# A six-part decoder on one core: three bias additions as TensorE products with a row of ones, the gated experts copied out of PSUM by ScalarE, and softplus compensation without a scale

## The reference, cut to what matters

```python
# L0_ffn: two dense experts, each kept where the gate's top-2 picks it
e0 = silu(x @ w0.T + b0); e1 = silu(x @ w1.T + b1)
out = e0 * fw[:, 0:1] * m0 + e1 * fw[:, 1:2] * m1
# L1_attn: state-space mixer
projected = h @ in_proj_w.T + in_proj_b;  x, z = split(projected, 2)
x = silu(conv(x) + conv_b);  dt, Bc, Cc = split(x @ x_proj_w.T, ...)
dt = softplus(dt @ dt_proj_w.T + dt_proj_b)
decay = floor(exp(dt * A) * 2**15) / 2**15          # 512 channels x 16 states
h = decay * h + (x * Bc) * dt                       # scan over 256 positions
y = (h * Cc).sum(states) + x * D;  y = y * silu(z)
out = y @ out_proj_w.T + out_proj_b
# L1_xattn: 8 heads of 64 against a context of 256 positions
out = softmax(q @ k.T * scale) @ v @ Wo + bo
```

## Time and profile before

| what | value |
|---|---|
| median of 3 runs | 2634.4 us (2625.34 to 2636.75) |
| profiled execution | 2631.68 us, its span 2629.8 us |
| TensorE matmul busy over the span | 2168.8 us (82%), 11024 instructions |
| VectorE busy | 1634.4 us (62%) |
| ScalarE busy | 1030.7 us (39%) |
| GpSimd busy | 289.7 us (11%) |
| mean granted TensorE clock | 0.890 |

### The profile page before, as it was taken

One profiled execution on the slowest core, in us unless ns is written; L12 is line 12 of the kernel. 1 busy time (PEld: TensorE's weight loads), 2 busy tenths in 40 slices (PEclk: granted clock), 3 DMA queues, 4 the chain that ended last, 5 costly groups with the idle time before them and its releaser, 6 DMA issues. The chain is left out here.

```text
span 2629.8 us, 31266 instructions
## 1 busy us (share of the span) xinstructions
PE 2168.8 (82%) x11024; PEld 1327.3 (50%) x11024; DVE 1634.4 (62%) x2717; ACT 1030.7 (39%) x1611; POOL 289.7 (11%) x332
## 2 busy tenths in 40 slices
PE   6999999999999988754668887977888778749994
PEld 4666666666666655431323344434444434536662
DVE  6555555555555566447999999999999952120002
ACT  1222222222222222115765867587668712212220
POOL 1111111111111111100000000010000002110005
PEclk8999999999999999867779987988899876559997
DMA  6000100010001000010110111111001120003333
GB/s 219 1 0 17 46 2 0 17 41 8 0 17 41 7 0 0 1 40 33 54 49 23 47 40 38 34 38 37 27 33 55 48 68 30 15 19 100 100 100 112
DMA packets 57469, 102.55 MB, mean 39 GB/s; under 512 B 7828, under 2 KB 39087, under 8 KB 56832
## 3 DMA queue, kind: packets, MB, share of 16 engines
q1 hardware_dynamic: 54272, 93.67, 10.8%
q0 software_dynamic: 3072, 7.28, 0.9%
HBM read 87.10 MB, written 14.94 MB: 39 GB/s over the span
## 5 line engine op out<-in xcount | busy, mean ns | idle before, releaser
L1788 PE MATMUL pa<-arena 128*128 128x512 f32 x512 | 306.4, 728 | 97.7 <-DVE arena L1363 97.5
L1355 DVE TENSOR_TENSOR_SCAN arena<-arena 128x1024 f32<-128x1024 f32 x128 | 292.3, 2284 | 8.4 <-ACT arena L813 8.0
L1576 PE MATMUL po<-arena 128*128 128x256 f32 x1024 | 230.1, 381 | 0.0
L1566 PE MATMUL pa<-arena 128*128 128x512 f32 x512 | 227.9, 598 | 0.8 <-ACT arena L661 0.8
L1788 PEld LDWEIGHTS pa<-arena 128*128 128x128 f32 x512 | 103.4, 221 | 228.8 <-DVE arena L1363 127.5
L676 ACT COPY arena<-po 128x512 f32<-128x512 f32 x64 | 37.5, 586 | 462.6 <-PE po L1531 462.6
L1576 PEld LDWEIGHTS po<-arena 128*128 128x128 f32 x1024 | 191.2, 189 | 31.9 <-issue 3.5
L528 POOL TENSOR_SCALAR arena<-arena 128x2 f32<-128x2 f32 (+1 forms) x92 | 27.5, 299 | 1602.4 <-DVE arena L1222 932.0
L797 ACT ACTIVATE arena<-arena 128x510 f32<-128x510 f32 x256 | 170.4, 716 | 59.1 <-DVE arena L1355 51.5
L1497 PE MATMUL po<-arena 128*128 128x128 f32 x492 | 94.0, 326 | 117.5 <-ACT arena L824 74.9
L1052 DVE TENSOR_TENSOR arena<-pa,arena 128x512 f32<-128x512 f32 x256 | 158.4, 681 | 25.9 <-PE pa L1511 25.0
(11 more groups left out here) (254 smaller groups left out, 3701.0 us busy)
## 6 DMA issues: line engine op xcount, KB each, us to landing
arena<-bc_rows SPq DMA_DIRECT2D x64, 512.0 KB, 4.4
arena<-in_L_ffn_W SPq DMA_DIRECT2D x16, 1024.0 KB, 7.3
arena<-in_L_attn_W SPq DMA_DIRECT2D x8, 1024.0 KB, 5.2
rows_to_experts<-arena SPq DMA_DIRECT2D x4, 1024.0 KB, 12.6
arena<-rows_to_experts SPq DMA_DIRECT2D x8, 512.0 KB, 8.5
rows_from_experts<-arena SPq DMA_DIRECT2D x8, 512.0 KB, 3.3
arena<-in_x SPq DMA_DIRECT2D x4, 512.0 KB, 6.8
arena<-in_rows SPq DMA_DIRECT2D x8, 256.0 KB, 3.2
```

What stands on the lines that cost most here:

```text
L1355: v.tensor_tensor_scan(h.rearrange(flat), decay.rearrange(flat), h.rearrange(flat), 0.0, ALU.mult, ALU.add).then_inc(scan_done, 1)
L1566: last = mm(pa[(i + 2) % 4][:, :], w1[:, k, ts(i, P)], yT[:, k, :], start=k == 0, stop=k == KC - 1)
L1576: last = mm(po[s][:, ts(i, D)], gT[:, c, ts(2 * s + i, P)], w2[:, c, :], start=c == 0, stop=c == FM - 1)
L1788: last = mm(pa[c][:, :], ident, uh[i % len(uh)][:, n, :], start=g == 0 and n == 0, stop=g == NS // NG - 1 and n == NG - 1)
```

## The change

TensorE gets a helper `biased`, a product of one row of ones with one row of the bias, which opens an accumulation; the products that follow add to it. It is used for the gated experts, the output projection and `w_o`. VectorE's three bias additions go. The experts' PSUM tile is now copied out by ScalarE in slots 15 to 18, so the table `HEAD` has five As where it had Vs, and silu waits for all four copies. Waits on the semaphore `xc_ready` become waits on `proj_added`. In softplus the correction is subtracted as it is; the factor 0.5 e - 1 and the product with it go (two operations over 128 x 2048), and the last operation subtracts instead of adding.

```diff
-HEAD = "AAAAAAVVAAVVVVVAA"
+HEAD = "AAAAAAVVAAVAAAAAA"
@@ SyncE
-        sp.wait_ge(xc_ready, PAIRS)
+        sp.wait_ge(proj_added, 2 * PAIRS)
@@ ScalarE
+            def expert_out(i):
+                nc.scalar.copy(eb[:, i, :], part(11 + i)).then_inc(head_a, 1)
+
             def experts_silu():
+                act.wait_ge(head_a, HEAD_A * n + 12)
                 for i in range(TT):
-                    act.wait_ge(head_v, HEAD_V * n + 4 + i)
                     a_(eb[:, i, :], eb[:, i, :], ACT.Silu).then_inc(sil_ready, 1)
...
+                if 15 <= i < 19:
+                    expert_out(i - 15)
                 if i == 19:
                     experts_silu()
@@ VectorE
-            def pair_biased(i):
-                v.tensor_tensor(eb[:, i, :], part(11 + i), r_pair, ALU.add).then_inc(head_v, 1)
...
-                step.after(v.tensor_scalar(soft_r, soft_e, 0.5, -1.0, ALU.mult, ALU.add))
                 dve.wait_ge(soft_u_ready, 2 * n + 2)
                 step.after(v.scalar_tensor_tensor(soft_e, soft_d, 1.0, soft_e, ALU.subtract, ALU.subtract))
-                step.after(v.tensor_tensor(soft_e, soft_e, soft_r, ALU.mult))
                 dve.wait_ge(relu_ready, IC * n + IC)
-                step.after(v.tensor_tensor(dt, dt, soft_e, ALU.add))
+                step.after(v.tensor_tensor(dt, dt, soft_e, ALU.subtract))
...
-                dve.wait_ge(proj_added, 2 * p + 2)
-                v.tensor_tensor(pair, pair, wide(r_out, TT), ALU.add).then_inc(xc_ready, 1)
-                hold(dve, xc_ready, p + 1)
+                hold(dve, proj_added, 2 * p + 2)
                 statistics(rows)
             if q is not None:
                 cross(UNITS + 3)
-                dve.wait_ge(wo2_out, 4 * q + 4)
-                step.apart(v.tensor_tensor(xst[:, ts(q, TT), :], xst[:, ts(q, TT), :], wide(r_xo, TT), ALU.add))
...
             if q is not None:
+                hold(dve, wo2_out, 4 * q + 4)
                 statistics(rows_of(q))
@@ TensorE
+        def biased(bank, bias):
+
+            mm(bank, ones[0:1, :], bias[0:1, :], start=True, stop=False)
...
             def expert_pair(i):
                 bank = part(11 + i)
+                biased(bank, r_pair)
                 for c in range(KC):
-                    last = mm(bank, xnT[:, c, ts(i, P)], w_pair[:, c, :], start=c == 0, stop=c == KC - 1)
+                    last = mm(bank, xnT[:, c, ts(i, P)], w_pair[:, c, :], start=False, stop=c == KC - 1)
...
                     pe.wait_ge(at2T_out, 4 * q + tile + 1)
                     pe.wait_ge(pexp_ready, 16 * q + min(4 * tile + 6, 16))
+                    biased(bank_score[:, 0:D], r_xo)
                     for c in range(QC):
-                        last = mm(bank_score[:, 0:D], at2T[:, c, :], w_o[:, c, :], start=c == 0, stop=c == QC - 1)
+                        last = mm(bank_score[:, 0:D], at2T[:, c, :], w_o[:, c, :], start=False, stop=c == QC - 1)
...
                     for i in range(2):
+                        biased(proj_banks[s][:, ts(i, D)], r_out)
                         for c in range(IC):
-                            last = mm(proj_banks[s][:, ts(i, D)], dtx[:, c, ts(2 * s + i, P)], w_out[:, c, :], start=c == 0, stop=c == IC - 1)
+                            last = mm(proj_banks[s][:, ts(i, D)], dtx[:, c, ts(2 * s + i, P)], w_out[:, c, :], start=False, stop=c == IC - 1)
```

More of the change, by code:

```diff
@@ L48 @@
 END_STEPS = 5
-HEAD_STEPS, TAIL_STEPS, CROSS_STEPS = 47, 5, 22
+HEAD_STEPS, TAIL_STEPS, CROSS_STEPS = 45, 5, 21
 ACT_STEPS = 2 * UNITS
@@ L292, in decoder @@
     xpad = arena[:, units_at:units_at + IC * 2 * (S + KCONV - 1)].rearrange("p (c s t) -> p c s t", c=IC, s=2)
-    soft_e, soft_l, soft_d, soft_r = chunks_at(units_at), chunks_at(units_at + IC * W), dtx, chunks_at(late + 2 * NG * W)
+    soft_e, soft_l, soft_d = chunks_at(units_at), chunks_at(units_at + IC * W), dtx
     qT, kT, vv = a(QC, W), a(QC, W), a(TT, QI)
@@ L360, in decoder @@
     w_in_2, ctx_in, a_exp, a_ready = sem("w_in_2"), sem("ctx_in"), sem("a_exp"), sem("a_ready")
-    xn_ready, xc_ready, xf_kept = sem("xn_ready"), sem("xc_ready"), sem("xf_kept")
+    xn_ready, xf_kept = sem("xn_ready"), sem("xf_kept")
     ctxn_in, head_done, head_a, head_v = sem("ctxn_in"), sem("head_done"), sem("head_a"), sem("head_v")
@@ L1298, in head @@
                     gate_logits()
-                if i == 14:
-                    pair_biased(0)
                 if i == 15:
                     gate_weights()
-                    pair_biased(1)
-                if i in (16, 17):
-                    pair_biased(i - 14)
                 if i == 19:
@@ L1334, in cross @@
                     if tile == 0:
-                        dve.wait_ge(xc_ready, q + 1)
+                        dve.wait_ge(proj_added, 2 * q + 2)
                     v.tensor_tensor(row_of, bank_score[:, 0:D], row_of, ALU.add).then_inc(wo2_out, 1)
@@ L1423, in mixer @@
             if p is not None:
-                rows, pair = rows_of(p), xst[:, ts(p, TT), :]
+                rows = rows_of(p)
                 for s in range(2):
```

## The result

| | before | changed |
|---|---|---|
| median, 10 runs each | 2636.0 us (nine from 2625.3 to 2640.9, one of 6986.5) | 2652.5 us (2640.0 to 2659.4) |
| ratio, 95% interval | | 1.0058 (1.0034 to 1.0081) |
| profiled span | 2629.8 us | 2638.2 us |
| VectorE busy | 1634.4 us | 1603.4 us |
| TensorE busy, instructions | 2168.8 us, 11024 | 2207.6 us, 11120 |

What follows compares the result with a forecast made beforehand. VectorE bounds within a scan, the TensorE-ScalarE chain between scans. Pass terms 1.9 - 1.7 + 0 + 1.9 + 0.3 + 1.3 = +3.7 us on 2634.4 gave 2638; forecast 2637 us, range 2612 to 2649.

Steps and rivals of the forecast that it cites:

- The price of a bias product: On TensorE, a one-row product costs 0.93 us for 512 columns, 0.45 for 256, twice that at the lower clock.
- the terms that the products make: Parts of the pass sums that fall away if bias products are free: 14.8 us in all, 2.6 of it in pass 6.
- Pass 1, +1.9: Head with nothing beside it: additions start 5.4 us later behind copies and table load, softplus gives back 3.55; sum +1.9 us.
- the TensorE term of 3.5 us: Pass 1: eight more instructions for the experts, 0.44 us each at the higher clock, end them 3.5 us later.
- Pass 2, -1.7: Four units lose 0.6 us each, -2.4; behind the scan TensorE's longer run makes scan 2 come 0.7 later; sum -1.7 us.
- Passes 3 and 4, 0 and +1.9: Tile waits for w_o and TensorE's run 2.25 us longer behind the scan, partly taken up by idle: sums 0 and +1.9 us.
- Pass 5, +0.3: Two tiles' waits add 0.9 us; in the tail the output projection grows 1.8, the chain is 0.6 shorter; sum +0.3.
- Pass 6, +1.3: Pure chain at clock 0.58: waits for tiles 1 to 3 add 2.6 us, the last bias addition's removal saves 1.3; sum +1.3.
- A: Faster rival, passes 1 to 6: VectorE is the bound and most of its 34.9 us come through, 2611 us; chance 0.22.
- B: Slower rival: TensorE at the lower clock in slots 13 to 16 of passes 3 and 4, 24 to 40 us, about 2665; chance 0.12.
- C: Rival: as forecast, but the added products cost nearly nothing, 11 us less, 2623 us; chance 0.06.
- The other two signs: Wrong if scans of passes 3 to 5 start earlier after the previous scan, or TensorE's clock in passes 3 and 4 moves over 0.03.

Runs made afterwards that it cites:

- the kernel with 128 rows: The changed kernel with each bias product made as identity times the bias tile, 128 rows in place of one: 2634.2 us, ratio 1.0003 to the kernel before.
- changed again: The changed kernel, nothing edited, run once more for a second profile and more times: 2653.8 us, ratio 1.0075 to the kernel before.

## Why the prediction was wrong, point by point

- **The price of a bias product: the step that failed.** "I take a product's time as independent of its rows", and its upper bound was the same figure: "nothing, if one row were free, and these figures". The support was the earlier trace rows: 64 rows take as long as 128. But each of these two groups stands behind a change of the row count, so both lengths, 3.70 and 3.71, hold the same share of its price (eight without a change take 3.60, below), and comparing them can't show it. The price is 0.83 us for 256 columns, not 0.45, 1.25 for 512, not 0.93, and 1.46 at w_o and half clock, not 0.9. With the price restored to 0.43 the kernel takes 2634.2 us, where 2637 was forecast. The trace of before did hold the price. Four instructions of 512 columns without a change behind them come in 1.72 us (1424.65 to 1426.37); among the keys, which alternate between 128 and 64 rows, four take 2.11 (1440.80 to 1442.91): 0.39 for two changes.

```profile
1424.65 1.88 PE L1755 MATMUL pa<-arena 128*128 128x512 f32 x4
1426.37 3.60 PE L1931 MATMUL pa<-arena 128*96 128x512 f32 x8
...
1440.80 1.13 PE L1838 MATMUL po<-arena 128*128 128x512 f32 x2
1441.85 1.12 PE L1839 MATMUL po<-arena 64*128 64x512 f32 x2
1442.91 1.13 PE L1838 MATMUL pt<-arena 128*128 128x512 f32 x2
```

- **How much of the products stays hidden.** A second term was mis-sized, and an opposite one hid it. For passes 1 to 5 the terms that the products make were 12.2 us (14.8 less 2.6 in pass 6); at the price that the prediction assumed they are 18.3. Without the products the same passes were to win 9.8 us and won 18.2. So the sum took too little for the products and too little for VectorE's savings. That the kernel with 128 rows comes within 3 us of the forecast is in part luck: its passes 3 to 5 are -5.2, -0.8 and +5.2, where 0, +1.9 and +0.3 were forecast.
- **Pass 1, +1.9**, was +5.4 and +5.6. The chain was right (experts later, copy, table load, silu, then the additions). The additions start 6.8 and 7.1 us later against the cut, not 5.4, since the TensorE term of 3.5 us was too small: to the next product it is 1.05 us for three of the four and 2.0 for the first, at half clock, and the products behind them are slower too. From there to the first scan, which softplus was to shorten by 3.55, it is only 1.4 and 1.5 us less. With 128 rows pass 1 is +2.7.
- **Pass 2, -1.7.** The four units give back 2.4 us, exactly as worked out. Behind the scan +0.7 was forecast; it is +0.6 with 128 rows and +2.2 with one in the first profile: four times 0.4. The second profile has +3.3 for the whole pass.
- **Passes 3 and 4, 0 and +1.9.** The run from the output projection to the end of w_o grew by 4.0 us, not 2.25. With 128 rows the passes are -5.2 and -0.8, so here I was also too dark about what VectorE's savings give (1.7 of the 5.2 us are TensorE's clock behind pass 3); the two errors had opposite signs, and the price was the larger.
- **Pass 5, +0.3.** +7.1 and +0.6 in two profiles of one program. The kernel before was fast here in its one profile: softplus alone, which adds nothing, is +3.8 too.
- **Pass 6, +1.3**, is +1.3 in the second profile, but by luck: it starts at a higher clock (0.76 against 0.70), so tile 0's addition comes 3.4 us earlier, and from there to tile 3's it takes 76.1 us in place of 70.1, where +2.6 was forecast. The output bias alone, without a product here, has 74.3. In the first profile the short form hides it.
- **The rivals.** A (VectorE's savings arrive) had 2611. It needs the products to be gone, not only cheap: with 48 of them at the low price the time is 2634.2, without them 2610.9. B gave a slower kernel, by TensorE at the lower clock in slots 13 to 16; there the experts' products ran at the higher clock (four instructions in 1.99 us in all slots of passes 3 and 4), so its direction came by another cause. C (free products) had 2623; with the products left out it is 2610.9, so that sum was 12 us too dark.
- **What would show it wrong** named "a one-row product takes a fraction of 0.45 us", below the price alone. I had looked for a cheap product, never for a dear one. The other two signs did not come either: the first scans of passes 3 to 5 start 50.0, 59.5 and 57.5 us behind the last scan before them, where it was 50.1, 58.9 and 55.5, and the clock of passes 3 and 4 stays 0.88.

## What to carry to other kernels

Before a bias goes to TensorE, look at the row counts of its neighbours: a product with another row count than the products around it pays for two changes, and on a path where TensorE is late this is more than the addition that it saves. A product with all 128 rows (the identity times the replicated bias) does the same at half the price. And an upper bound that equals the estimate is no bound: for an operation that the trace doesn't show, look for the nearest place where the pattern, not only the operation, occurs.

## What the hardware showed unexpectedly

**Pass 6 has a short and a long form, about 10 us apart.** In the changed kernel's two profiles it takes 148.2 and 159.2 us. The difference is made in its first 34 us, and it goes with the granted clock: 0.95 in the short one, 0.76 in the long one, and 0.70 in the profile of before. The stretches (start:end, length, busy us, clock), before, changed, and changed again:

```profile
2174.45:2208.45 34.00, 30.05 (x73) 15.54 (x74) 10.16 (x26) 8.82 (x22) 0.00 (x0) 0.70 0.00 0
```

```profile
2191.54:2225.54 34.00, 28.02 (x96) 14.02 (x96) 14.83 (x49) 11.01 (x29) 0.10 (x1) 0.95 0.00 0
```

```profile
2195.85:2229.85 34.00, 29.78 (x83) 16.07 (x83) 12.79 (x39) 8.81 (x22) 0.00 (x0) 0.76 0.00 0
```

In the first two TensorE comes from the same work at the same lower clock (0.50 in the 12 us ahead of the cut), and does 96 instructions in one and 73 in the other. GpSimd's scatter then starts 33.9 us behind the cut in place of 40.4. The other engines stall beside that scatter (VectorE for 23.1 us in the kernel before); in the short form tile 0's addition gets through ahead of the stall, at 50.0 us, and in the long one behind it, at 74.6. Six of the thirteen profiles have the short form, all six with a clock of 0.95 there; the seven long ones have 0.70 or 0.76. These kernels have no edit in common, and which form an execution takes was not explained. The changed kernel's ten times lie in two groups, 2640 to 2645 us with a mean clock of 0.894 to 0.896 over the execution, and 2651 to 2659 us with 0.889 to 0.892. That fits the two forms, but no times of single passes exist for them. So a median over few runs can hold some us of this, whatever the edit.
